# Two attention layers of a 4096-token block: scores from two float32r halves in 64-row tiles instead of three bf16 parts in 99 rows, with PSUM dealt out anew

## What is computed

```python
def _msa(x, w_qkv, w_proj):                 # H = 16 heads, DK = 8
    qkv = (x @ w_qkv).reshape(b, n, 3, H, DK)
    ...
    attn = jnp.einsum('bhnd,bhmd->bhnm', q, k) * (1.0 / np.sqrt(DK))
    attn = jax.nn.softmax(attn, axis=-1)
    y = jnp.einsum('bhnm,bhmd->bhnd', attn, v)
    ...
x = x + 0.5 * _L0_ffn_ref(_layernorm(x), ...)
x = x + _L0_attn_ref(_layernorm(x), ...)    # the recurrence
x = x + 0.5 * _L0_ffn_ref(_layernorm(x), ...)
```

## Time and profile before

| | |
|---|---|
| time, median of 3 runs | 1777.81 us (1775.66 to 1779.79) |
| the profiled execution's own time | 1772.23 us |
| its span, first to last instruction | 1770.5 us |
| granted clock of TensorE, mean | 0.853 of 2.4 GHz |
| PE busy | 1338.7 us (76%) |
| DVE busy | 1133.6 us (64%) |
| ACT busy | 892.5 us (50%) |
| POOL busy | 613.4 us (35%) |
| first attention phase | about 111 to 536 us |
| second attention phase | about 1125 to 1553 us |

### The profile page before, as it was taken

How to read it: one execution, slowest core, us unless ns; L and a number is a source line. 1 busy time by engine, 2 the same in 40 slices (tenths; PEclk the granted TensorE clock), 3 DMA queues, 4 the chain that set the end, 5 groups by cost and what they waited for, 6 DMA issues and landing times. The chain is left out here.

```text
span 1770.5 us, 35271 instructions
## 1 busy us (share of the span) xinstructions
PE 1338.7 (76%) x10520; PEld 662.6 (37%) x10521; DVE 1133.6 (64%) x1595; ACT 892.5 (50%) x1764; POOL 613.4 (35%) x981
## 2 busy tenths in 40 slices
PE   3249999999996239438888737499999999861394
PEld 1112333333326239414545434123333333261394
DVE  7347888888846313448878759477888888462132
ACT  3225777777773025224343415267777777730252
POOL 5351111111112356435747537511111111134453
PEclk9567999999996569759899956689999999975697
DMA  6851212212102112200000002512122122021123
GB/s 191 159 131 33 54 44 54 52 44 54 51 5 78 37 50 68 66 0 3 2 4 3 2 1 71 125 29 56 45 51 55 44 51 55 2 84 35 49 68 111
DMA packets 124561, 93.69 MB, mean 53 GB/s; under 512 B 15994, under 2 KB 120157, under 8 KB 124465
## 3 DMA queue, kind: packets, MB, share of 16 engines
q1 hardware_dynamic: 113584, 81.04, 17.8%
q0 software_dynamic: 6656, 9.28, 1.7%
q10 hardware_dynamic: 4224, 2.10, 0.4%
HBM read 54.75 MB, written 29.43 MB: 48 GB/s over the span
## 5 line engine op out<-in xcount | busy, mean ns | idle before, releaser
L720 DVE TENSOR_REDUCE maxima<-ps 128x2 f32<-128x1024 f32 x512 | 603.0, 1220 | 122.5 <-PE ps L599 122.5
L701 ACT ACTIVATE probs<-ps 128x512 f32<-128x512 f32 x1024 | 556.9, 598 | 178.4 <-PE ps L607 177.5
L607 PE MATMUL ps<-q_stack,k_stack 99*128 99x512 bf16 x1024 | 322.7, 388 | 8.4 <-ACT probs L701 5.4
L599 PE MATMUL ps<-k_stack,q_stack 96*128 96x512 bf16 x1024 | 280.9, 396 | 39.5 <-DMA k_stack<-k_split 34.9
L614 PE MATMUL ps<-probs,v_stack 128*32 128x512 f32 x2048 | 274.5, 608 | 1.9 <-ACT probs L701 1.9
L607 PEld LDWEIGHTS ps<-q_stack,k_stack 99*128 99x128 bf16 x1024 | 85.9, 97 | 295.4 <-ACT probs L701 245.0
L599 PEld LDWEIGHTS ps<-k_stack,q_stack 96*128 96x128 bf16 x1024 | 98.5, 99 | 164.3 <-DMA k_stack<-k_split 35.3
L550 POOL DMA_DIRECT2D q_stack<-max_rows x64 | 42.8, 669 | 313.0 <-ACT max_rows L682 313.0
L1083 DVE COPY w_now<-w 128x512 f32 x80 | 34.3, 429 | 148.8 <-issue 77.7
L558 POOL TENSOR_SCALAR neg_rest<-maxima 128x16 f32<-128x16 f32 x64 | 16.0, 249 | 304.2 <-DVE maxima L720 304.2
L1064 ACT ACTIVATE xT<-ps,ln_b,ln_w 128x128 f32<-128x128 f32 x80 | 36.7, 458 | 158.0 <-PE ps L1035 158.0
(11 more groups left out here) (225 smaller groups left out, 1892.4 us busy)
## 6 DMA issues: line engine op xcount, KB each, us to landing
q_stack<-q_split SPq DMA_DIRECT2D x192, 96.0 KB
k_stack<-k_split SPq DMA_DIRECT2D x128, 64.0 KB
q_split<-q_parts SPq DMA_DIRECT2D x16, 384.0 KB, 2.4
k_split<-k_parts SPq DMA_DIRECT2D x16, 384.0 KB, 2.5
k_stack<-k_split SPq DMA_DIRECT2D x64, 96.0 KB
sorted<-rows SPq DMA_DIRECT2D x10, 516.0 KB, 11.6
xt<-sorted SPq DMA_DIRECT2D x80, 64.5 KB, 1.8
k_stack<-k_split SPq DMA_DIRECT2D x128, 32.0 KB
```

Source lines behind the costliest of these rows:

```text
L599: last = t.matmul(psS[:, h, :], qs[g][0:MAXROW, h, u * P:(u + 1) * P], ks[g][0:MAXROW, h, :], start=True, stop=True)
L607: t.matmul(psE[:, h % 2, :], ks[g][0:STACK, h, u * P:(u + 1) * P], qs[g][0:STACK, h, :], start=True, stop=True).then_inc(e_ready, 1)
L701: a.activation(probs[u % 2][:, h, :], psE[:, h % 2, :], ACT.Exp, scale=float(DK) ** -0.5).then_inc(e_read, 1)
L720: v.tensor_reduce(maxima[i][:, 2 * pair:2 * pair + 2, u:u + 1], psS[:, 2 * pair:2 * pair + 2, :], AX_X, ALU.max).then_inc(s_read, 1)
```

## The change

Q and K are cut into two float32r parts instead of three bf16 ones: ACT copies the first, DVE's difference is already the second, and what ACT and POOL did for the third part is gone. A head's stack is 4 pairs of parts times 8 = 32 rows, then 30 rows of zeros against ones, then two rows for the maximum: 64 rows. Even heads stand in rows 0 to 63, odd heads in rows 64 to 127. S takes 62 rows, E takes 64. PE's order in a unit becomes S0, E, S1, E, (turns), S2, E, S3, PV, E, where E takes the heads in the order 1, 0, 3, 2, so that neighbours S and E lie in different halves of the array. PSUM: four banks for S as before, three banks (a ring) for E and the two turns, one bank for PV's output. The turns are of full float32 and ahead of PV. The maxima come negated out of DVE, POOL splits them in two instructions instead of five, and two DMAs place them instead of one. The loads are 12 DMAs a group instead of 8, and the stacks are filled with constants at the start by 8 POOL and 8 DVE instructions instead of 8 and 4. The loads no longer wait for that; PE does.

```diff
-SPLITS = 3
+F32R = mybir.dt.float32r
+
+SPLITS = 2
 ROWS = SPLITS * SPLITS * DK
-MAXROW = 96
-STACK = MAXROW + SPLITS
-TWO_ONES = 1.0 + 0x3F80 * 2.0 ** -23
+
+
+HALF = 64
+MAXROW = HALF - SPLITS
+STACK = HALF
...
-        parts = {k: sbs(k + "_parts", [P, SPLITS, SW], BF16) for k in "qk"}
-        rest = {k: sbs(k + "_rest", [P, SW]) for k in "qk"}
+        parts = {k: sbs(k + "_parts", [P, SPLITS, SW], F32R) for k in "qk"}
...
                             after(vec, high[k], j, 3)
-                            after(vec, low[k], j, 5)
-                            v.tensor_tensor(rest[k][o][:], psX[k][o], parts[k][o][:, 0, :],
-                                            ALU.subtract).then_inc(diff[k], 1)
+                            v.tensor_tensor(parts[k][o][:, 1, :], psX[k][o], parts[k][o][:, 0, :].bitcast(F32),
+                                            ALU.subtract).then_inc(low[k], 1)
...
-                    if present(3):
-                        for k in "qk":
-                            after(act, diff[k], j, 3)
-                            a.activation(parts[k][o][:, 1, :], rest[k][o][:], ACT.Copy).then_inc(mid[k], 1)
...
-                    if present(3):
-                        for k in "qk":
-                            after(pool, mid[k], j, 3)
-                            g.tensor_tensor(parts[k][o][:, 2, :], rest[k][o][:], parts[k][o][:, 1, :],
-                                            ALU.subtract).then_inc(low[k], 1)
...
-        qs = [sb(f"q_stack{i}", [P, GROUP, T], BF16) for i in range(NG)]
-        ks = [sb(f"k_stack{i}", [P, GROUP, T], BF16) for i in range(NG)]
...
+        qs = [sb(f"q_stack{i}", [P, PAIRS, T], F32R) for i in range(NG)]
+        ks = [sb(f"k_stack{i}", [P, PAIRS, T], F32R) for i in range(NG)]
...
+        maxima = [sb(f"maxima{i}", [P, 2, PAIRS, TPB]) for i in range(2)]
+        NMAX = 2 * SPLITS * PAIRS * TPB
+        neg_wide = sb("neg_wide", [P, P], F32R)
+        neg_parts = neg_wide[:, 0:NMAX].rearrange("p (e a m) -> p e a m", e=2, a=SPLITS)
+        max_rows = [sb(f"max_rows{i}", [P, P], F32R) for i in range(2)]
...
         psS = ps[:, 0:4, :]
-        psE = ps[:, 4:6, :]
-        psO = [ps[:, 6, :], ps[:, 7, :]]
...
+        RINGS, FIRST_RING = 3, 4
+        psO = ps[:, 7, :]
+        PER_LOAD = 16 * 12
+        PLACED = 16 * 2
+
+
+
+        E_ORDER = (1, 0, 3, 2)
+        RING = []
+        for u in range(TPB):
+            RING += [("e", u, 0), ("e", u, 1)]
+            if u == 1:
+                RING.append(("o",))
+            if u == 2:
+                RING.append(("m",))
+            RING += [("e", u, 2), ("e", u, 3)]
+        assert len(RING) % RINGS == 0
+
+        def ring(*user):
+            return ps[:, FIRST_RING + RING.index(user) % RINGS, :]
+
+        def half(h):
+            return slice(HALF * (h % 2), HALF * (h % 2) + STACK)
+
+        def score_rows(h):
+            return slice(HALF * (h % 2), HALF * (h % 2) + MAXROW)
...
+                    def rows(dram, first, count, e):
+                        heads = dram.rearrange("c (n p e) t -> c n p e t", p=PAIRS, e=2)
+                        return heads[first:first + count, g, :, e, ds(b * T, T)]
+
+                    for e in range(2):
+                        for a in range(SPLITS):
+                            row = HALF * e + a * SPLITS * DK
+                            sp.dma_start(qs[g][row:row + SPLITS * DK, :, :].bitcast(F32),
+                                         rows(qd, 0, SPLITS * DK, e)).then_inc(loaded[g], 16)
+                            for at in (row, row + DK):
+                                sp.dma_start(ks[g][at:at + DK, :, :].bitcast(F32),
+                                             rows(kd, a * DK, DK, e)).then_inc(loaded[g], 16)
...
                 for g in range(NG):
-                    sp.wait_ge(q_set, g + 1)
-                    sp.wait_ge(k_set[g // 2], g % 2 + 1)
                     load_group(0, g)
...
-                    g_.memset(in_pairs(qs[i][:]), 0.0).then_inc(q_set, 1)
+                    for e in range(2):
+                        g_.memset(qs[i][HALF * e + ROWS:HALF * e + MAXROW, :, :].bitcast(F32), 0.0).then_inc(q_set, 1)
+                pool.wait_ge(q_set, 2 * NG)
                 for i in range(NG):
...
+                    g_.memset(vs[i][:], 0.0).then_inc(v_set, 1)
+                g_.memset(neg_wide[:, NMAX:].bitcast(F32), 0.0).then_inc(v_set, 1)
...
-                                   max_rows[i][:]).then_inc(rows_placed, 16)
+                    for e in range(2):
+                        at, rows = HALF * e + MAXROW, SPLITS * PAIRS * TPB
+                        pool.dma_start(qs[g][at:at + SPLITS, :, :].bitcast(F32),
+                                       max_rows[i][e * rows:(e + 1) * rows, :].bitcast(F32)).then_inc(rows_placed, 16)
...
-                    g_.tensor_scalar(neg_rest[:], m, -1.0, None, ALU.mult).then_inc(split_step, 1)
-                    wait_apart(pool, pool_passed, (split_step, 4 * group + 1))
-                    g_.tensor_copy(neg_parts[:, 0, :], neg_rest[:]).then_inc(split_step, 1)
...
+                    g_.tensor_copy(neg_parts[:, :, 0, :], m).then_inc(split_step, 1)
+                    wait_apart(pool, pool_passed, (split_step, group + 1))
+                    g_.tensor_tensor(neg_parts[:, :, 1, :], m, neg_parts[:, :, 0, :].bitcast(F32),
                                      ALU.subtract).then_inc(split_done, 1)
...
+                def score(g, u, h, count):
...
-                    for h in (2 * pair, 2 * pair + 1):
-                        last = t.matmul(psS[:, h, :], qs[g][0:MAXROW, h, u * P:(u + 1) * P], ks[g][0:MAXROW, h, :],
-                                        start=True, stop=True)
-                    last.then_inc(s_ready, 1)
...
-                    if not (isinstance(count, int) and count < 2):
-                        pe.wait_ge(e_read, count - 1)
-                    t.matmul(psE[:, h % 2, :], ks[g][0:STACK, h, u * P:(u + 1) * P], qs[g][0:STACK, h, :],
+                    mm = t.matmul(psS[:, h, :], qs[g][score_rows(h), h // 2, u * P:(u + 1) * P],
+                                  ks[g][score_rows(h), h // 2, :], start=True, stop=True)
+                    if h % 2:
+                        mm.then_inc(s_ready, 1)
+
...
+                    at = RING.index(user) - RINGS
...
+                    before = RING[at]
+                    if before[0] == "e":
+                        pe.wait_ge(e_read, GROUP * TPB * group + GROUP * before[1] + before[2] + 1)
+                    elif before[0] == "o":
+                        pe.wait_ge(o_done, group)
+                    else:
+                        pe.wait_ge(rows_kept, group + 2)
+
+                def exponent(b, g, first, last, u, n):
+                    h = E_ORDER[n]
+                    ring_free(b, g, first, last, "e", u, n)
+                    t.matmul(ring("e", u, n), ks[g][half(h), h // 2, u * P:(u + 1) * P], qs[g][half(h), h // 2, :],
                              start=True, stop=True).then_inc(e_ready, 1)
...
-                def turn_max(g, count, *bank_free):
-                    wait_apart(pe, pe_passed, (split_done, count), *bank_free)
-                    t.transpose(psO[g % 2][0:SPLITS * NMAX, 0:P // 2].bitcast(BF16),
-                                neg_parts[:].rearrange("p c m -> p (c m)"), s["ident16"][:]).then_inc(rows_turned, 1)
...
+                def turn_max(count):
+                    pe.wait_ge(split_done, count)
+                    t.transpose(ring("m")[:, 0:P], neg_wide[:].bitcast(F32), s["ident"][:]).then_inc(rows_turned, 1)
...
+                pe.wait_ge(k_set, 2 * NG)
+                pe.wait_ge(q_set, 2 * NG)
+                pe.wait_ge(v_set, NG + 1)
...
+                        ahead_score(0)
+                        exponent(b, g, first, last, u, 0)
+                        ahead_score(1)
+                        exponent(b, g, first, last, u, 1)
+                        if u == 1 and not (first and g == 0):
+                            ring_free(b, g, first, last, "o")
+                            turn_o(G)
+                        if u == 2 and not (last and g == NG - 1):
+                            ring_free(b, g, first, last, "m")
+                            turn_max(G + 2)
+                        ahead_score(2)
+                        exponent(b, g, first, last, u, 2)
+                        ahead_score(3)
...
-                                if not (first and g < 2):
-                                    pe.wait_ge(rows_kept, G + 1)
-                                    pe.wait_ge(o_done, G - 1)
-                                else:
-                                    pe.wait_ge(rows_kept, G + 1)
+                                if not (first and g == 0):
+                                    pe.wait_ge(o_kept, G)
                             pv(g, u - 1, unit - 1)
...
                             pv((g - 1) % NG, TPB - 1, unit - 1)
```

(35 more changed lines are left out.)

123 lines of the change are left out of this document (45 added, 78 removed).

## The result

The changed kernel takes 1792.06 us (median of four runs, 1790.20 to 1796.69) against 1778.45 us for the kernel before (four runs on the same chip): a ratio of 1.0088, 95% interval 1.0063 to 1.0113: a small loss, but clear of the noise. The prediction was 1739 us and faster. The profiled execution has a span of 1789.4 us, before 1770.5: 18.9 us more. From the start of its first exponential to the start of its last, the first attention phase grew from 387.1 to 402.5 us and the second from 388.9 to 400.6, 27.1 us in all; everything else became 8.2 us shorter.

What follows compares the result with a forecast made beforehand. PE bound the old kernel, then a loop of waits would. Savings of 23.4 + 2 + 10 + 3.4 = 38.8 us off 1772.2 gave 1733.4, as run median 1739 us; own case 1712 to 1765, range 1688 to 1795.

Steps and rivals of the forecast that it cites:

- the third E and S3 follow each other: 0.22: Step of the unit's loop of waits: both are heads of the same half, so S3 starts 0.22 us after E.
- last E to its exponential: 0.42: Step of the unit's loop of waits: from the last E on PE to its exponential on ACT, 0.42 us.
- rivals 3 and 5: Attention: 3, halves do not run at once, 1775 us, chance 0.08; 5, tiling changes of 0.2 us, 1787, chance 0.07.
- PE no longer the bound, a loop of waits instead: Attention unit: PE's own work falls to 2.20 us from 2.88; a five-term loop of waits sets 2.61 us.
- The turns, 0.7 and 0.5: Units 1 and 2 of a group: turns of output and maxima make them 0.7 and 0.5 us longer.
- Placing the maxima, just in time: Attention group: the second placing DMA lands at 11.5 of 11.64 us; 0.06 us a group added for late landings.
- qkv phases, 10 us: Both qkv phases: shorter rounds and earlier last stores save 11.2 us, less 1 for larger stores: 10 us.
- The start of attention, 3.4 us: Start of both attention phases: fill 0.5 us less, split of the maxima 1.2 less, both twice: 3.4 us.
- 1 (a shorter loop): Attention's loop of waits is shorter than worked out: groups of 11.0 us, about 1697 us, chance 0.13.
- 2 (DVE as the bound): Attention: PE's scores are simply halved and DVE's 9.7 us is the group: about 1620 us, chance 0.04.
- 4 (slow products): S and E on PE: a float32r product takes longer than bf16, about 1890 us or 2400, chance 0.13.
- Rival 6 (clock): TensorE in attention: the clock falls to half, 16.5 us a group, 2040 us, chance 0.05.

Runs made afterwards that it cites:

- experiment 5: Changed kernel with S and E over all 128 rows, no 64-row tiles, exponentials taken with scale 0: 1821.9 us.
- experiments 4 and 8 to 10: Changed kernel with all S and E in the lower half: 2517.6 us; with S and E over 32 and 34, 34 and 36, 32 and 64 rows: 2977.16, 2234.87, 2959.9.
- experiment 9: Changed kernel with S contracting over 34 rows and E over 36, instead of 62 and 64: 2234.87 us.
- experiment 2: Changed kernel with the heads of E in order 1, 0, 2, 3, so the third E and S3 lie in different halves: 1750.56 us.

## Why the prediction was wrong

The step that failed is "the third E and S3 follow each other: 0.22", together with "last E to its exponential: 0.42". Both took rows of bfloat16 products whose weight load is short. Measured with float32r they are 0.34 and 0.53. I had seen the long records (0.19 us) and priced them at the wrong place: "if they hold a pair to 0.26 the unit's slack takes it". That was right for the pairs, which start 0.235 apart behind a load that ran ahead. But at the two places of the loop no load runs ahead. At the third E it has waited for the bank together with PE. At the last E it stands behind PV, in another tiling. Nothing is left there that could hide it, and 0.11 us is lost at each: a steady group took 12.53 us and not 11.70, with bfloat16 alone taken back 11.71.

In sum the miss is 57.7 us of the profiled execution (18.9 longer instead of 38.8 shorter). Attention grew by 27.1 where 25.4 less were forecast, 52.5 of the 57.7, and 60 x 0.83 = 50 of these are the steady groups. The qkv phases make 1.7, the start of attention 0.7; 2.8 lie elsewhere and were not looked into. The 1792 us lie inside the range of 1688 to 1795 only because it was stretched to rivals 3 and 5; the prediction's own case ended at 1765.

The Trainium skill, page "TensorE: Matmul & The Clock Gate", section Weight-path perf modes, says that the fast weight load is on for 128 weights and an input type that is not FP32. It does not say where float32r stands. In the trace the mean record of L619's load is 187 ns, like the 0.19 us of a float32 load, and 94 in the bfloat16 kernel: float32r loads as float32 does. That bears on the step that failed.

Point by point:

- *PE no longer the bound, a loop of waits instead*: right; all five terms were found at their places, three with the forecast numbers.
- *The turns, 0.7 and 0.5*: right, 0.68 and 0.49.
- *Placing the maxima, just in time*: it was better than that. The issues take 0.576 us (median) instead of 0.66 and the landing 1.9 instead of 2.2, and no E waits; 0.06 a group was not lost. In bfloat16 the group is 11.71 where 11.64 was worked out.
- *Groups without S, 2 us less*: no. In the first phase one takes 11.62 us, before 11.56; they hold the exposed load too (10.84 in bfloat16).
- *qkv phases, 10 us*: 8.3. In the second, from its start to attention's first fill 69.34 us instead of 75.85, 6.5 as forecast; in the first only 1.8 instead of about 4, since it starts again later after the constants' stall (a `zn` at 79.01 us, before at 76.37). Why it does was not tested.
- *The start of attention, 3.4 us*: 2.7. From the fill to the first S nothing was gained (10.28 in both phases, before 10.20 and 9.97), from the first S to the first exponential 1.6 in the first phase (21.03 instead of 22.62) and 1.5 in the second.
- *Float32r product at 0.22*: nearly, 0.235.

Of the rivals, 1 (a shorter loop) and 2 (DVE as the bound) fell with the group of 12.53, 3 (no overlap) with the pairs and with experiment 5, and 4 (slow products) with the 0.235. Rival 5 gave 1787, close to the result, by a price that isn't there: S3 to PV takes 0.33 us, 0.09 to 0.10 beyond the product, also with 128-row tiles, and in the same tiles with bfloat16 the group is 11.71. It was near in one thing: one of the two places lies at a change of tiling, and with float32r the exposed load is paid there. Rival 6 (clock) didn't come true, but I argued it from gaps between products; experiments 4 and 8 to 10 show that in this kernel it depends on the rows, which I had not weighed at all. It was nearer than its 0.05, and dearer: at half clock a group took 19.61 us in experiment 9, where it had 16.5.

## What to carry to other kernels

When a change halves the work of the full engine, write down the loop of waits that is left and price each of its steps with the new type, the weight load too: here a load was free only behind a product of the same tiling that was still running, never behind a wait or a change of tiling. Then move off the loop whatever needn't stand there; in this kernel one line moved was worth 42 us, the whole new order 69. And don't take rows of zeros for waste before a run without them.

## What the runs showed that I had not expected

- The granted clock of the steady stretch by the rows of its S and E: 96 and 99 rows (before) 1.00; 128 rows 1.00; 62 and 64 rows in both halves 0.99; 62 and 64 in one half alone 0.50; 34 and 36 in both halves 0.50; 32 with 34 or 64 in both halves 0.50. In all of them it stood at 0.50 from 130 to 140 us, in the first S; only with 96 and 99, with 128, and with 62 and 64 in both halves it rose behind that.
- Even with 62 and 64 rows the high clock is not certain: one of the four executions of experiment 2 took 2150.91 us at a mean granted clock of 0.545, the others 1749.37 to 1750.62 us at 0.851 to 0.854. The trace is of one of the others, so what held the clock down is open.
- A float32r load that can't run ahead costs 0.11 us, one of bfloat16 0.01 (a product's record is then 0.39 instead of 0.38 us); so the type decides what a wait or a change of tiling costs.
- Products of 32 and of 34 rows, or of 32 and 64, in different halves never overlap (0.72 us apart at 1.2 GHz); 34 and 36, and 62 and 64, start within 0.01 us of each other.
- Halving PE's share of S and E by overlap brought 30 us of 1822; moving one S ahead of one E brought 42.
